# A four-layer graph network on one core: splitting VectorE's dependent steps, moving small sums to GpSimd and norms and a relu to ScalarE, with a new merged order

## What is computed

```
x = layernorm(x + L0(x, adj))   # two-layer graph convolution on 5 groups of the first 25 nodes, summed
x = layernorm(x + L1(x, adj))   # 8-head attention: softmax(q k / 4 + log(adj + 1e-6)) v, then Wo and bo
x = layernorm(x + L2(x, adj))   # relu(dinv * adj * dinv * (x W^T + b))
x = layernorm(x + L3(x, adj))   # 5 gated recurrent steps: m = h W_l; agg = A^T m; h = gru(agg, h)
```

## Time and profile before

| what | value |
|---|---|
| median of 3 runs | 1811.12 us (1809.5 to 1811.14) |
| time of the profiled execution | 1810.14 us |
| its span | 1808.3 us |
| mean granted TensorE clock | 0.966 |
| busy: TensorE matmul / weight load | 91% / 75% |
| busy: VectorE / ScalarE / GpSimd | 82% / 66% / 41% |

### The profile page before, as it was taken

The page is one execution under the profiler, slowest core; times in us unless marked ns, Lnnn a source line. Parts: engine busy times, 40 slices in busy tenths (PEclk is TensorE's granted clock), DMA queues, the critical chain, the costliest instruction groups (busy, mean ns, idle before and its releaser), DMA issues.

```text
span 1808.3 us, 33536 instructions
## 1 busy us (share of the span) xinstructions
PE 1652.4 (91%) x12060; PEld 1355.1 (75%) x12060; DVE 1485.2 (82%) x3979; ACT 1187.1 (66%) x2738; POOL 733.1 (41%) x619
## 2 busy tenths in 40 slices
PE   4779999999999989999998999999899999989885
PEld 3567788787877878777887877788787778877763
DVE  5576897979889797988979798897979889787864
ACT  1455677676667767666776766768676677766652
POOL 1133343535334353543435344343534434343431
PEclk8899999999999999999999999999999999999997
DMA  3000100101010010101001010100101010000000
GB/s 86 20 22 19 28 18 11 37 13 28 24 28 14 12 40 13 28 24 28 13 13 40 13 28 24 29 13 13 40 13 28 24 28 13 13 25 13 13 7 12
DMA packets 84798, 40.90 MB, mean 23 GB/s; under 512 B 10629, under 2 KB 84634, under 8 KB 84634
## 3 DMA queue, kind: packets, MB, share of 16 engines
q1 hardware_dynamic: 84250, 38.64, 7.7%
...
q10 hardware_dynamic: 384, 0.13, 0.0%
...
## 4 chain that ended last, share of the span: by engine, by line
PE 61%; DVE 23%; ACT 10%; issue 3%; SPq 0%; POOL 0%; DMA 0%; DVEq 0%; POOLq 0%; ACTq 0%
PE RA L869 12%; PE RB L869 11%; PE Q L836 7%; PE RT L1045 6%; ACT e_s L537 5%; PE RT L836 4%; DVE stats L590 4%; PE Q L972 3%; PE Q L1003 3%; PE M L904 2%; PE M L912 2%; DVE tr L759 2%; DVE mv L593 2%; PE Q L987 2%; PE Q L955 2%
## 5 line engine op out<-in xcount | busy, mean ns | idle before, releaser
L472 POOL TENSOR_TENSOR h_lo<-hT,h_hi 128x512 fp32r<-128x512 f32 x160 | 204.7, 1280 | 573.4 <-ACT h_hi L559 483.6
L537 ACT ACTIVATE e_s<-Q,s_ng 128x128 f32<-128x128 f32 x1024 | 297.1, 409 | 17.6 <-DVE s_ng L707 17.4
L440 POOL TENSOR_TENSOR rs<-ve,half_neg 128x4 f32<-128x4 f32 x128 | 148.4, 1159 | 318.6 <-DVE ve L595 318.6
L475 POOL TENSOR_TENSOR hd<-hT,nn 128x512 f32<-128x512 f32 x160 | 221.5, 1385 | 41.1 <-ACT nn L571 40.7
L707 DVE TENSOR_REDUCE s_ng<-Q 128x4 f32<-128x512 f32 x256 | 170.5, 683 | 17.3 <-PE Q L972 16.7
L565 ACT ACTIVATE tr<-RA,b_rz 128x512 f32<-128x512 f32 x160 | 114.8, 717 | 104.3 <-PE RA L869 104.3
L713 DVE TENSOR_TENSOR p_s<-Q,adjTe 128x512 f32<-128x512 f32 x256 | 172.3, 683 | 11.8 <-PE Q L836 11.5
L571 ACT ACTIVATE nn<-tr,wT 128x512 f32<-128x512 f32 x160 | 118.3, 740 | 89.7 <-DVE tr L759 88.7
L836 PE MATMUL Q<-ident,e_s 128*128 128x128 f32 x1024 | 156.5, 279 | 11.5 <-ACT e_s L537 11.4
L755 DVE SCALAR_TENSOR_TENSOR un<-tr,un 128x512 f32<-128x512 f32 x160 | 110.3, 689 | 66.1 <-ACT un L568 62.3
L869 PE MATMUL RB<-h_hi,whh_hi 128*128 128x512 f32 x320 | 145.6, 455 | 11.2 <-ACT tz L574 11.2
...
## 6 DMA issues: line engine op xcount, KB each, us to landing
...
adjc<-in_adj_dram SPq DMA_DIRECT2D x128, 4.0 KB, 1.8
...
```

Source lines behind the costliest of these rows:

```text
L440: return pool.tensor_tensor(r[:, :], v[:, :], half_neg[:, 0, 0:GB], ALU.pow)
L472: pool.tensor_tensor(h_lo[g][:, :], hT[g][:, :], h_hi[g][:, :], ALU.subtract).then_inc(SG["h_lo"][g], 1)
L475: pool.tensor_tensor(hd[g][:, :], hT[g][:, :], nn[g][:, :], ALU.subtract).then_inc(SG["hd"][g], 1)
L537: ins = act.activation(e_s[:, j, c, :], Q[j][:, c * P:(c + 1) * P], ACT.Exp, bias=s_ng[:, j, c:c + 1])
```

## The change

1. VectorE's chains are cut into steps of their own in the table. `u` (reciprocal) and `n` (division) are apart, so that both reciprocals come ahead of both divisions. `h_new` is divided into `he` and `h_new`. `l0_prep` becomes `l0_dinv`, `l0_mask`, `l0_row`, `l0_turn`, `l0_col` and `l0_nat`. Each `bn_stats` has its own semaphore count, and each `bn_aggr` waits for its own `bn_stats` alone.
2. GpSimd takes the addition of 1e-5 (`above`) of all four norms and the two guards of the degree (`deg == 0` and the sum), each with a wait on GpSimd's own semaphore ahead of the power.
3. ScalarE takes the last step of the third and the fourth norm as four activations `y * rs + nm`, for which VectorE computes `nm = -mean * rs` (`shift`, 128x4), and the relu of L2 as four activations. ScalarE then also waits for the output's store (`out_done`).
4. All four tables of `MERGE` are new; the steps of each thread keep their order.

```diff
-    vector=("RARBAAARBRRBARAABRARAARAARRAAARARRBRARRRRBBRRARAAAARRRRBRRBRRAABARBBRAARARARRAARRRRAARARRARB",
+    vector=("AARRARBBRABARRAAARBARRRAARRAAARRARRBARBRRRRBBBRBAARRRBAARRBRAARARBABRBRRARABARARRARRBAARRRRRAAARARRRRABA",
...
-    return out + [(*at, "u", 0), (*at, "u", 1), (*at, "on", 0), (*at, "wo", 0)]
+    return out + [(*at, "u", 0), (*at, "u", 1), (*at, "n", 0), (*at, "n", 1), (*at, "on", 0), (*at, "wo", 0)]
...
-        return [(*pair, "l0_deg", 0), (*last, "x2", 0), *second, (*pair, "l0_prep", 0), (*end, "x1", 0),
+        return [(*pair, "l0_deg", 0), (*last, "x2", 0), *second, (*pair, "l0_dinv", 0), (*pair, "l0_mask", 0), (*pair, "l0_row", 0),
+                (*pair, "l0_turn", 0), (*pair, "l0_col", 0), (*pair, "l0_nat", 0), (*end, "x1", 0),
...
-            out += [(*before[:2], "h_new", before[2])]
+            out += [(*before[:2], "he", before[2]), (*before[:2], "h_new", before[2])]
...
+            def above(m, v):
+
+                return pool.tensor_scalar(v[:, :], m[:, :, 1], 1.0, LN_EPS, ALU.mult, ALU.add)
...
-                    wait(pool, "l0_prep", it, 5)
+                    wait(pool, "l0_deg", it, 3)
+                    pool.tensor_scalar(cols(deg0_z), cols(deg0), 0.0, None, ALU.is_equal).then_inc(S["l0_safe"], 1)
+                    wait(pool, "l0_safe", it, 1)
+                    pool.tensor_tensor(cols(deg0_s), cols(deg0), cols(deg0_z), ALU.add).then_inc(S["l0_safe"], 1)
+                    wait(pool, "l0_safe", it, 2)
...
-                    wait(pool, "ln1", it, 3 * g + 3)
+                    wait(pool, "ln1", it, 2 * GB * (g + 1))
+                    above(mv[g][0], ve[g][0]).then_inc(S["ln1_eps"], 1)
+                    wait(pool, "ln1_eps", it, g + 1)
                     root(ve[g][0], rs[g][0]).then_inc(S["ln1_pow"], 1)
...
-                    wait(pool, "deg", it, 3 * g + 3)
+                    wait(pool, "deg", it, g + 1)
+                    pool.tensor_scalar(deg_z[g][:, :], deg[g][:, :], 0.0, None, ALU.is_equal).then_inc(S["deg_safe"], 1)
+                    wait(pool, "deg_safe", it, 2 * g + 1)
+                    pool.tensor_tensor(deg_s[g][:, :], deg[g][:, :], deg_z[g][:, :], ALU.add).then_inc(S["deg_safe"], 1)
+                    wait(pool, "deg_safe", it, 2 * g + 2)
                     root(deg_s[g], deg_p[g]).then_inc(S["deg_pow"], 1)
...
+            def normalise(o, y, r, n):
+                for b in range(GB):
+                    ins = act.activation(o[:, b, :], y[:, b, :], ACT.Identity, bias=n[:, b:b + 1], scale=r[:, b:b + 1])
+                return ins
...
+                elif kind == "out":
+                    wait_g(act, "nm4", g, it, 1)
+                    act.wait_ge(out_done[g], (it + 1) * 16)
+                    normalise(x4[g], y4[g], rs4[g], nm4[g]).then_inc(SG["x4"][g], 1)
+
+                elif kind == "x3":
+                    wait_g(act, "nm3", g, it, 1)
+                    normalise(x3[g], y3[g], rs[g][2], nm3[g]).then_inc(SG["x3"][g], 1)
+
+                elif kind == "l2_agg":
+                    wait(act, "a_mm", it, g + 1)
+                    wait(act, "dinv", it, g + 1)
+                    if it + g > 0:
+                        wait(act, "y3", it + g - 1, 2 - g)
+                    for b in range(GB):
+                        ins = act.activation(a_r[:, b, :], M2[:, b * P:(b + 1) * P], ACT.Relu, scale=dinv[g][:, b:b + 1])
+                    ins.then_inc(S["a_relu"], 1)
...
                 for b in range(GB):
-                    ins = dve.bn_stats(st[:, b, :], y[:, b, :])
-                at(ins, 1)
+                    mark(dve.bn_stats(st[:, b, :], y[:, b, :]))
                 for b in range(GB):
-                    ins = dve.bn_aggr(m[:, b, :], st[:, b, :])
-                at(ins, 2)
-                at(dve.tensor_scalar(v[:, :], m[:, :, 1], LN_EPS, None, ALU.add), 3)
+                    reach(b + 1)
+                    mark(dve.bn_aggr(m[:, b, :], st[:, b, :]))
 
...
+            def shift(o, m, r):
+                return dve.scalar_tensor_tensor(o[:, :], m[:, :, 0], -1.0, r[:, :], ALU.mult, ALU.mult)
...
-                    wait(dve, "deg", it, 3 * g + 1)
-                    dve.tensor_scalar(deg_z[g][:, :], deg[g][:, :], 0.0, None, ALU.is_equal).then_inc(S["deg"], 1)
-                    wait(dve, "deg", it, 3 * g + 2)
-                    dve.tensor_tensor(deg_s[g][:, :], deg[g][:, :], deg_z[g][:, :], ALU.add).then_inc(S["deg"], 1)
...
                     dve.reciprocal(den[:, k, :, :], o4[:, :, :, DH]).then_inc(S["den"], 1)
+                elif kind == "n":
                     wait(dve, "den", it, PAIRS * g + k + 1)
+                    o4 = Q[1 + k][:, :].rearrange("p (a h d) -> p a h d", a=2, h=HEADS)
...
                 elif kind == "l2_agg":
-                    wait(dve, "a_mm", it, g + 1)
                     wait(dve, "x2", it, g + 1)
-                    dve.scalar_tensor_tensor(a_r[:, :, :], M2[:, :].rearrange("p (b d) -> p b d", b=GB), 0.0,
-                                             per_graph(dinv[g][:, :]), ALU.max, ALU.mult).then_inc(S["a_relu"], 1)
...
-                    normalise(x3[g], y3[g], mv[g][2], rs[g][2]).then_inc(SG["x3"][g], 1)
+                    shift(nm3[g], mv[g][2], rs[g][2]).then_inc(SG["nm3"][g], 1)
...
-                elif kind == "h_new":
+                elif kind == "he":
                     wait_g(dve, "hd", g, it, k + 1)
                     wait_g(dve, "z_act", g, it, k + 1)
                     dve.scalar_tensor_tensor(hd[g][:, :], tz[g][:, :], 1.0, hd[g][:, :], ALU.add, ALU.mult).then_inc(SG["he"][g], 1)
+                elif kind == "h_new":
...
-                    dve.wait_ge(out_done[g], (it + 1) * 16)
-                    normalise(x4[g], y4[g], mv4[g], rs4[g]).then_inc(SG["x4"][g], 1)
+                    shift(nm4[g], mv4[g], rs4[g]).then_inc(SG["nm4"][g], 1)
```

115 lines of the change are left out of this document (62 added, 53 removed).

## The result

The changed kernel takes **1731.46 us** (median of 4 runs, 1731.03 to 1732.58) where the kernel before takes 1811.13 on the same chip; the ratio is 0.9562, 95% interval 0.9545 to 0.9578. The profiled execution took 1731.32 us. The forecast was 1769 with a range from 1732: the sign is right, but the gain is nearly twice as large as forecast (80 us against 42) and just outside the range.

A forecast was written before the change was run, and what follows sets the result against it. TensorE bounds the rounds, so only its waits and the clock lost by waiting can go. Fifteen rounds at -2.95 us make -44, the ends +2: 1810.1 becomes 1768 profiled, 1769 us median; range 1732 to 1806.

The forecast's parts named there:

- Term A: End of the second half: TensorE's standing and lost clock fall from 6.4 to 3.95 us, -2.4 us a round.
- Term B: Middle of the second half: the hn gate's 0.95 us goes, ScalarE backlog adds 0.4, so -0.55 us a round.
- Term C: First half: `on_ts` covered, 0.3 us gained; last `p` group has less time, 0.3 lost; sum 0.
- term D: First and last rounds, where norms are serial: longer chains add +2 us in all, bounds 0 and +6.
- The walk: Engine times stepped through the second half's end in the new order: 3.95 us of TensorE standing left, in five pieces.
- its own list: Work taken from VectorE per round (norm steps, relus, additions of 1e-5, guards): 7.5 us, from 91.5 to 84.
- Its sign on the wait for `xT`: With norm groups of 1.64 us on ScalarE, the wait for `xT` would be 0.3 us longer, the forecast 4 us later.
- rival 1: Whole round: more waiting goes than walked, VectorE's backlog being overstated; 1703 us if all, 1735 half way; chance 0.20.
- Rival 2: End of the second half: TensorE's clock still falls, so 1.6 us a round stays, 1792 us; chance 0.12.
- Rival 3: Both halves: ScalarE becomes the chain and the kernel slower, 1863 us if all uncovered, 1825 at 60%; chance 0.13.

The follow-up runs named there:

- first attempt at a better order: Changed kernel with product with v and `o_ts` ahead of the r gate, `a_bin` and statistics behind the divisions, fourth norm's last step in the next half: 1799.09 us.

## Why the prediction was right in sign and wrong in size

**What bounds.** Right: TensorE bounds, its work did not change, and the gain is what it no longer waits for. The wait for `o_ns` was the largest piece, and went.

**The step that failed** is the size of the four terms of the sum. In the prediction's own terms, for a round: A -2.4, measured -3.2; B -0.55, measured -0.95; C 0, measured -0.4; everything else 0, measured -0.4. And term D for the ends +2, measured about -5. All err to the same side.

**Term A.** The walk's order and its pieces are right, each within 0.5 us: the turn ahead of `end` at 6.04 (forecast 6.0), `o_ts` transposes at 8.6 (8.6), 4.8 + 1.6 down to 3.2 in all. That the turn fits to 0.04 is in part luck: the first norm's chain started 0.4 us later than walked and took 1.77 us instead of 2.1. What was mis-sized is VectorE's backlog from the end of a set to the last division, which ended at 10.87 instead of 11.3, so that `on` follows the z gate without its 0.5. The walk let the end of a set take 2.5 us, as before (2.55). It takes 2.22: 0.20 of the difference is the addition of 1e-5, which the walk left in though its own list takes it off VectorE (with the sums back it is 2.42), and 0.13 is the divided chain (joined it is 2.35). `nm` comes 0.3 earlier by this, and so do `on_ts` and `xT`.

**Term B.** The hn gate's wait is gone, as forecast, but ScalarE had no backlog: the r gate's tanh is ready 4.5 us behind the z gate, so the 0.4 did not come. **Term C:** `on_ts` gained what was forecast, and the last `p` group lost nothing. Another 0.4 us is spread over gaps below 0.2; what gives them no run isolates.

**Term D.** Fifteen rounds of 4.93 make 74 of the 78.8 us between the two spans; 4.8 us more came off the serial head and tail, although GpSimd's additions and the longer norm groups stand there. Which of the moves does that, no run isolates, so this part stays open.

**What is taken from VectorE.** The busy time is as forecast (91.5 to 84.1), but two omissions nearly cancel. 2.0 us of the 84.1 are the two instructions a round that run as long as GpSimd's `hd`, which the prediction did not have; without them VectorE would be at 82.1. And 1.4 us came off by the divided chains, which the forecast did not count in this sum. The sentence "almost none of it is on the path by itself, since TensorE hides it; it counts where VectorE is late" holds for the old order, by the run with the new work alone. In the new order the runs price the parts by their place and not by their length: the sums, 3.5 us a round, 3.04; the relus, 1.4 us, 2.93; the norms, 3.8 us by durations, 0.57.

**ScalarE.** Norm groups take 1.65 us, the forecast had 1.5 and as upper bound 1.6. The prediction's estimate from the Trainium skill (ScalarE: Activation LUTs, What ACT_TABLE_LOAD costs) was 1.64 us, and the trace agrees with it. Its sign on the wait for `xT` did not come, since VectorE's earlier end outweighed it.

**GpSimd.** The additions take 0.26 us on average (0.19 and 0.28 at the place of the walk), the degree guards 0.4, about within the bounds of 0.2 and 0.69, and in the full rounds nothing waits for them. What the prediction left out is that GpSimd's `hd`, which was there before, now meets small VectorE instructions in time.

**The rivals.** The result lies at rival 1 (more goes than walked; 5.2 a round and 1735 were its half way). It named the cause of the error in term A, a walk that overstates VectorE's backlog; its many small waits are only the 0.4 us spread over the round. It deserved more than 0.20. Rival 2 (the clock still falls) did not come: the pieces of standing that are left, none above 1.2 us, leave it at 1.00. The rival was real: with 1.63 us for `o_ns` the clock falls in 12 of 12 rounds (first attempt at a better order), with 2.21 in 9 of 12. Rival 3 is real in the old order: 1867 us. That this is near its 1863 is luck, since it took all of ScalarE's added time as uncovered and set the gains of the new order against it.

The sum of what was mis-sized: 2.0 us a round over 15 rounds are 30 us, the ends 7, together the 37 us between 1768 and 1731.
